# A softmax attention's last unit sums over all 512 queries in one set of products instead of two

## What is computed

```python
q = apply_rope(q)
k = apply_rope(k)
q = q * (1.0 / jnp.sqrt(jnp.float32(hd)))
scores = jnp.einsum('bhqd,bhkd->bhqk', q, k)
attn = jax.nn.softmax(scores, axis=-1)
out = jnp.einsum('bhqk,bhkd->bhqd', attn, v)
out = out.transpose(0, 2, 1, 3).reshape(B, S, d)
attn_out = out @ Wo + bo
x = x + attn_out
x_norm2 = layer_norm(x, g2, beta2)
ffn = jax.nn.relu(x_norm2 @ W1 + b1) @ W2 + b2
return x + ffn
```

## Time and profile before

| | us |
|---|---|
| median of 3 runs | 953.96 |
| lowest and highest | 953.88, 955.05 |
| the profiled execution | 953.76 |
| its span in the trace | 951.9 |
| last unit, key tile 3 to the copy of the last sums | 663.22 to 679.56 |

### The profile page before, as it was taken

One profiled execution on the slowest core, in us unless ns is written; L12 is line 12 of the kernel. 1 busy time (PEld: TensorE's weight loads), 2 busy tenths in 40 slices (PEclk: granted clock), 3 DMA queues, 4 the chain that ended last, 5 costly groups with the idle time before them and its releaser, 6 DMA issues.

```text
span 951.9 us, 17381 instructions
## 1 busy us (share of the span) xinstructions
PE 828.7 (87%) x6615; PEld 530.3 (56%) x6615; DVE 664.3 (70%) x1288; ACT 555.1 (58%) x1205; POOL 198.3 (21%) x177
## 2 busy tenths in 40 slices
PE   4889937799999889999999999999995899895894
PEld 2579735599956543333333333333575598594694
DVE  5855884266567999999999999992427364566362
ACT  2451542155525856999999888899644254423252
POOL 2000037455500050000000000000112454205385
PEclk9999957999999999999999999999996799995897
DMA  4750001321130000000000000000230212000444
GB/s 122 200 142 1 1 14 48 106 67 35 38 91 1 1 1 1 2 1 2 1 2 2 1 2 1 2 2 1 89 91 15 90 39 75 2 1 31 125 36 71
DMA packets 54643, 36.86 MB, mean 39 GB/s; under 512 B 9138, under 2 KB 50162, under 8 KB 54546
## 3 DMA queue, kind: packets, MB, share of 16 engines
q1 hardware_dynamic: 47218, 25.98, 9.8%
q0 software_dynamic: 7344, 9.77, 4.4%
HBM read 22.31 MB, written 14.48 MB: 39 GB/s over the span
## 4 chain that ended last, share of the span: by engine, by line
DVE 33%; PE 32%; POOL 14%; issue 11%; DMA 4%; ACT 4%; SPq 1%; POOLq 0%; DVEq 0%; ACTq 0%
DVE arena L1634 22%; POOL slots L1147 7%; POOL results L1158 5%; PE psum L1718 4%; PE psum L1687 2%; POOL results L1169 2%; PE psum L1251 2%; ACT arena L1898 2%; PE psum L280 2%; PE psum L402 2%; PE psum L380 2%; PE psum L1781 2%; PE psum L1769 1%; PE psum L1616 1%; PE psum L440 1%
## 5 line engine op out<-in xcount | busy, mean ns | idle before, releaser
L1634 DVE TENSOR_REDUCE arena<-psum 128x2 f32<-128x1024 f32 x256 | 294.1, 1220 | 8.6 <-PE psum L1616 8.6
L1898 ACT ACTIVATE arena<-psum 128x512 f32<-128x512 f32 x512 | 266.7, 606 | 18.9 <-PE psum L1687 16.7
L1294 ACT ACTIVATE arena<-psum,arena 128x128 f32<-128x128 f32 x340 | 97.2, 369 | 122.2 <-PE psum L1261 65.7
L1718 PE MATMUL psum<-arena 128*32 128x256 f32 (+1 forms) x1920 | 159.6, 405 | 0.2 <-ACT expert_w L1879 0.2
L1687 PE MATMUL psum<-arena 32*128 32x512 f16 x512 | 127.3, 384 | 1.8 <-ACT arena L1898 0.4
L287 PE MATMUL psum<-la_wqkv,ident 128*128 128x384 f32 x336 | 123.5, 518 | 2.4 <-ACT arena L1998 2.0
L1616 PE MATMUL psum<-arena 32*128 32x512 f16 x512 | 100.6, 384 | 17.1 <-DVE arena L1634 15.1
L1147 POOL DMA_INDIRECT slots<-xn,arena x64 | 66.4, 1038 | 196.0 <-DVE arena L1371 177.4
L1251 PE MATMUL psum<-arena 128*128 128x128 f32 x680 | 97.0, 288 | 0.7 <-DVE arena L1452 0.6
L287 PEld LDWEIGHTS psum<-la_wqkv,ident 128*128 128x128 f32 x336 | 65.1, 202 | 52.2 <-issue 15.4
L1261 PE MATMUL psum<-arena 128*128 128x128 f32 x680 | 89.9, 275 | 1.0 <-ACT arena L1294 1.0
(11 more groups left out here) (279 smaller groups left out, 1074.7 us busy)
## 6 DMA issues: line engine op xcount, KB each, us to landing
arena<-slots SPq DMA_DIRECT2D x19, 256.0 KB, 3.0
arena<-results SPq DMA_DIRECT2D x12, 256.0 KB, 4.0
slots<-blank SPq DMA_DIRECT2D x1, 2560.0 KB, 11.8
expert_w<-in_L_attn_b_w_dram SPq DMA_DIRECT2D x1, 2048.0 KB, 8.4
expert_w<-in_L_attn_b_w_dram SPq DMA_DIRECT2D x8, 256.0 KB, 4.9
expert_w<-in_L_ffn_W_dram SPq DMA_DIRECT2D x1, 2048.0 KB, 8.6
expert_w<-in_L_ffn_W_dram SPq DMA_DIRECT2D x8, 256.0 KB, 5.0
results<-arena POOLq DMA_INDIRECT x85, 2.3
```

What stands on the lines that cost most here:

```text
L1294: last = nc.scalar.activation(self.hT[:, p, c, :], ps[:, 2 + p, c * P:(c + 1) * P], self.func, bias=own[:, FF + c:FF + c + 1])
L1634: v.tensor_reduce(self.mx[:, h % 2, keys, qt, 2 * pair:2 * pair + 2], core.psum[:, 2 * slot:2 * slot + 2, :], AX.X, ALU.max).then_inc(self ...
L1718: last = nc.tensor.matmul(core.psum[32 * j:32 * j + 32, 7, cols], self.vs[:, b * TB + kt, HG * g + j, :], self.prob[:, k % self.PROBS, j, ...
L1898: nc.scalar.activation(self.prob[:, k % self.PROBS, j, :], core.psum[:, 4 + tile % self.SCORE_BANKS, :], ACT.Exp).then_inc(self.prob_in, 1)
```

## The change

In the last unit (`h == HALVES - 1`) the sums of every key tile are made over all 512 queries at once, in the place of part 0, and part 1 is empty. `wave` is called from the same places as before.

```diff
         b, g, _ = self.half_of(h)
+        at_once = kt == 0 or h == self.HALVES - 1
         if part == 0:
             pe.wait_ge(self.prob_in, self.tile_of["score", k, HG - 1] + 1)
             if kt == 0 and h:
                 pe.wait_ge(self.sum_out, h)
-        if kt == 0 and part == 1:
+        if at_once and part == 1:
             return
-        cols = slice(256 * part, 256 * part + 256) if kt else slice(0, 512)
+        cols = slice(0, 512) if at_once else slice(256 * part, 256 * part + 256)
         for j in range(HG):
             last = nc.tensor.matmul(core.psum[32 * j:32 * j + 32, 7, cols], self.vs[:, b * TB + kt, HG * g + j, :],
-                                    self.prob[:, k % self.PROBS, j, cols], start=(kt == 0), stop=(kt == TB - 1 and part == 1))
-        if part == 1 or kt == 0:
+                                    self.prob[:, k % self.PROBS, j, cols], start=(kt == 0), stop=(kt == TB - 1 and (part == 1 or at_once)))
+        if part == 1 or at_once:
             last.then_inc(self.wave_in, 1)
```

## The result

| | before | changed |
|---|---|---|
| median of 6 runs, us | 954.16 | 950.42 |
| lowest and highest | 952.24, 955.81 | 949.69, 950.84 |
| the profiled execution | 953.76 | 950.56 |
| its span | 951.9 | 948.8 |

The ratio is 0.9969, with an interval of 0.9955 to 0.9982: faster by 1.7 to 4.3 us. Forecast were 952.5 us, a gain of 1.5 us, and a range from 951.5 us. The time lies outside the range, on the fast side.

A forecast was written before the change was run, and what follows sets the result against it. PE was taken to set the last unit's pace; with shorter key tiles and ScalarE's end then later, the copy of the sums starts 1.46 us earlier: 953.76 to 952.30 us, median 952.5 us, range 951.5 to 953.5 us.

The forecast's parts named there:

- the wait of score 3: Last unit, each key tile: score 3 waits 0.25 us for ScalarE to empty a bank; whole sums would remove this.
- signs of being wrong: Whole sum over 1.14 us, ScalarE waiting for PE ahead of the copy, or time before gate products moved under 1.2 us.
- the wait that I put at 0.17 us: Key tile 4, last unit: score 1 waits 0.17 us for a bank, since ScalarE started late at key tile 3.
- The price of 0.14 us for a key tile: Sums in the last unit: one whole sum takes 1.00 us against 1.14 us for two halves.
- the tail: Sums of key tiles 6 and 7 behind the loop: 1.98 us if nothing is gained (taken), 1.70 us at best.
- a loss of 0.1 us: Behind the loop: VectorE's normalisation moves 1.0 us against PE's 1.46 us, losing at most 0.1 us.
- The clock rival: Second expert block's gate products: the clock's fall comes behind them, another 0.65 us goes, 951.8 us; chance 0.2.
- The stall: Second pair of scores still takes 0.57 us, key tiles 3 to 6 give only 0.14 us each, 953.4 us; chance 0.12.
- ScalarE's end: 2.06 us stay between last exponential and copy, so only 1.03 us is won, 952.9 us; chance 0.14.
- The drain: Table switch ahead of the square root: the skill's 1380 ns drain would put the copy at about 679.5, gaining next to nothing.
- the slower rival: Last unit: ScalarE sets the pace, each of five key tiles costs 0.43 us, 2.15 us in all, 956.1 us; chance 0.03.
- the circle through the banks: Last unit: the next key tile's score 1 needs score 2's bank, free 2.45 us after the first pair of scores.

The follow-up runs named there:

- halves_together: Kernel before, last unit: both halves of the sums kept, the second right behind the first, ahead of score 2; ratio 1.0002, last copy 17.29 us after unit 14's.
- tail_only: Changed kernel with only key tiles 6 and 7, behind the loop, summed whole and 1 to 5 in halves; last copy 19.05 us after unit 14's (before 19.06).
- widen_first: Changed kernel with PE's second turning of the attention output moved behind the network's first four products; ratio 0.9982 to the kernel before.
- loop_only: Changed kernel with only key tiles 1 to 5 summed whole, 6 and 7 in halves; last copy 17.27 us after unit 14's (before 19.06).
- half_between: Kernel before, last unit: second half of the sums between score 2 and score 3; key tile 5 3.17 us, last copy 19.15 us after unit 14's.

## Why the prediction was wrong

**The mechanism held, in its place and nearly in its size.** In the profile of the changed kernel, by the prediction's own list: whole sums took 1.00 us (forecast 1.00); the wait of score 3 was gone; the key tiles were 2.35, 2.75, 2.72, 2.22 us (2.28, 2.90, 2.73, 2.22); the square root was followed by the copy with no idle time of ScalarE (so forecast); the copy came 1.80 us earlier (1.46). By its signs of being wrong it holds too: a whole sum cost less than 1.14 us, ScalarE did not wait for PE ahead of the copy, and the gate products start 1.31 us nearer to unit 14's copy (55.68 us, before 56.99 us).

**The terms that were mis-sized inside it.** Key tile 4 takes 2.75 us instead of 2.90, with less of the wait that I put at 0.17 us (its sums start 0.35 us behind its scores, 0.03 us more than without a wait). Key tile 3 took 0.07 us more than I had. In key tile 7 the wait is 0.16 us and not 0.23:

```profile
674.34 0.55 PE L1687 MATMUL psum<-arena 32*128 32x512 f16 x2
...
674.82 1.07 PE L1720 MATMUL psum<-arena 128*32 128x512 f32 x8
```

The third exponential starts 0.42 us behind its scores at the end (675.82 to 676.24), and I had 0.48 us. Together the last exponential ends 13.02 us after key tile 3 starts, not 13.25 us. And the copy starts 0.20 us behind the start of the square root, where I let it wait for the root's end, 0.32 us. These two make 0.35 us, and 0.34 us is what the forecast of the copy was short by.

**Merging.** The price of 0.14 us for a key tile was right, its reason was not: I read it as the gain of one product of 512 columns over two of 256. `halves_together` and `tail_only` show that it is the gain of sums that follow sums. For the tail I had taken nothing, between nothing and 0.28 us; nothing was right (1.92 against 1.93 us).

**Behind the loop** I allowed a loss of 0.1 us, and it was 0.50 us. I had seen that the normalisation on VectorE moves by the square root's gain and not by PE's, and held its end against PE. That cost 0.14 us. I did not follow VectorE's program one step on: the reading of the last turned outputs stands behind the normalisation, and PE's last turning waits for it. The stretch with this wait is 0.37 us longer. `widen_first` shows that the wait is there, and that taking it away by itself brings only 0.07 us at the end. The two errors, +0.34 and -0.40 us, nearly cancel, which is luck: forecast 1.36 to 1.46 us, measured 1.30 us at the network and 1.29 us at the next expert block's first scatter (68.91 against 67.62 us).

**The step that failed is the last one, from the gain of the stretch to the time of the kernel.** The sum put everything outside the stretch at no change, and the scatter between executions entered the range of 951.5 to 953.5 us only as three runs showed it (953.88 to 955.05 us). In the two first profiles the spans differ by 3.1 us, and only 1.3 us of it is the stretch. 0.66 us are the gate products, during which the clock fell in the one profile and not in the other; 2.2 us lie behind the next expert block's first scatter (221.8 against 219.6 us); and 1.1 us go the other way, ahead of unit 14's copy. The executions of the kernel before spread from 952.24 to 955.81 us in six runs, and from 952.96 to 959.87 us in 29.

1.3 us below 954 us is inside the range, and it is where the mechanism puts the changed kernel. Its first six runs lay around 950.4 us, and its 36 later ones around 955 us, beside a kernel before at 956 to 958 us. So the first measurement was on the fast side of the scatter, and the forecast was not missed by its mechanism. Why those six lie so low and so near together (949.69 to 950.84 us, all below the lowest of the later 36, 950.88 us) stays open; the short times of 11.50 and 11.99 us in the first expert block may belong to it, but only one execution of each kernel was profiled there. My estimate from these spreads, made afterwards, is that a range should have reached 3 us to either side.

That a faster stretch brings faster transfers behind it is neither shown nor excluded. From the next expert block's first scatter to the end, the seven profiles with the gain (the changed kernel's four, `halves_together`, `loop_only`, `widen_first`) took 219.5 to 223.9 us, 221.2 us on average; the five without it 220.7 to 224.6 us, 222.7 us on average. The difference of 1.5 us is within what such ranges leave open, and `half_between`, which gains nothing, took 220.7 us.

**The rivals.** The clock rival came true in the profile and not as an effect: the gate products took 3.65 us at a clock of 1.00 in the changed kernel's profile against 4.31 us at 0.83, but the kernel before has 3.65 us at 1.00 too, in its second profile. Even with it the prediction's time was 951.8 us, above what was measured. The stall did not stay. ScalarE's end did not keep its 2.06 us: from the last exponential's end to the copy it took 1.52 us (677.32 to 678.84). The drain that the Trainium skill (ScalarE: Activation LUTs, What ACT_TABLE_LOAD costs) counts beside the load does not show here either: the load starts 0.02 us behind the last exponential, and the root 0.02 us behind the load. ScalarE as the bound, the slower rival, is wrong in unit 15. In unit 14 alone whole sums cost 1.40 us, and in the units before it up to 1.68 us each, below the 2.15 us that the rival gave, and by the circle through the banks, in which ScalarE has idle time too. The clock stayed at 1.00 through PE's wait of 0.82 us.

## What to carry to other kernels

Where two kinds of product alternate on PE and a consumer frees the banks, look first at the order: a pair that goes together costs as much as one of it alone, and a wait for a bank disappears when enough other work stands ahead of it. The same order loses where no such work fills the round, so it belongs only where the trace shows the engine with more to do than the circle through the banks takes. And before a range is set for a kernel with gathers and scatters, ask on more than three runs how far executions of the same kernel lie apart, and judge a gain of 1 us by distances between two instructions of the trace.

## What the runs showed of the hardware

A product with 512 columns and two with 256 take PE nearly the same time in a row (1.92 and 1.93 us for the last two key tiles, 1.00 and 1.01 us for one key tile); the instructions saved are worth 0.01 us here. One more kind of work between two halves costs 0.13 us. A small ScalarE operation (square root of 128x8, 0.30 us) lets the next one start 0.20 us after its own start. For the same instructions, the time from the first expert block's last token scatter to its first result scatter ranged from 11.50 to 16.65 us between profiles. The gate products took 3.65 us at a granted clock of 1.00 and 4.31 us at 0.83.
